# The attention phase of a decoder layer: its ring of PSUM uses on seven banks instead of eight

## The chip, the cores and the metric

One Trainium2 chip, one of its cores. The time is the device time of one execution in microseconds (us), the median of several. Engines are called by the names of the profile: PE (TensorE matmuls), PEld (its weight loads), DVE (VectorE), ACT (ScalarE), POOL (GpSimd), SP (SyncE). PSUM, which PE writes and DVE and ACT read, has eight banks of 128 x 512 fp32 each in this kernel's tensor `ps`.

## The reference, cut to what matters

32 sequences of 128 tokens with 128 features, all fp32:

```
x = layernorm(x + attention(x))              # 16 heads of 64, causal, RoPE on half of each head
x = layernorm(x + cross_attention(x, ctx))   # 16 query heads of 8, 4 key/value heads, masks, RoPE
x = layernorm(x + moe_ffn(x))                # inner x added again; 8 experts, 256 wide, top 2
# attention:  softmax(mask(Q K^T) / 8) V, then W_o
# moe router: softmax-like gates by 3 Sinkhorn rounds over experts and tokens
# expert e:   (relu(x wg[e]) * (x wp[e])) wo[e]
```

## The kernel before, in words

There are two phases. The first does both attentions for all 32 sequences, the second (`ffn_phase`) the experts, in 8 groups of 4 sequences. The change touches the first alone; the second has rings of its own over the same PSUM tensor.

The attention phase is a software pipeline over sequences. `STAGE` gives four stages: f (transpose x, project to Q, K and V, RoPE, transpose heads), k (self-attention scores, softmax, times V, output projection), a (layernorm, cross-attention projections and scores) and c (cross-attention softmax times V, projection, layernorm, router logits). In slot s the sequence s is in stage f, s-1 in k, s-2 in a and s-3 in c. So slots run from 0 to 34: f is on in slots 0 to 31, k in 1 to 32, a in 2 to 33, c in 3 to 34. Slots 0 to 3 and 32 to 34 are written out, slots 4 to 31 are a hardware loop with two slots a turn.

Each engine has its work of a slot as a list in a fixed order (the functions `slot` in the blocks of sync, gpsimd, scalar, vector and tensor), and works it off in order. PE fills a bank, then ACT or DVE empties it. There are 40 such uses of a bank in a slot, listed in PE's order in the argument of `SlotRing`: `c.PT0`, `f.XT`, `c.PT1`, `c.PT2`, `k.S0`, `k.S1`, `f.Q0`, `a.T` and so on. The letter ahead of the point is the stage. Those that matter here:

- `f.XT` is the transpose of x by `x_transpose`, the second thing PE does in a slot. `f.Q0` to `f.Q5` are the projections (`qkv`, three matmuls each at L717 to L719).
- `k.S0` to `k.S3` are the self-attention scores. `scores(u)` fills two of them together and asks for both banks before it issues the first matmul (L738 and then L743). ACT's `exp_fill` empties them, with four exponentials and four reads of the accumulator each (L410), after DVE's `scores_max` (L516).
- `k.PT0` to `k.PT3` are the transposed probabilities (`prob_transpose`, L689), after POOL's `norm_fill` (L336). `k.OT0` and `k.OT1` are the products with V (`pv`, L763), `k.Y` the output projection (`out_proj`, 16 matmuls at L773), which DVE's `residual` (L531) reads.
- `a.QKV` is the cross-attention projection (`xqkv`, L786 and L787). `a.S0` to `a.S3` are the cross-attention scores (`xscores`, L802), emptied by ACT's `xexp_fill`, four exponentials each (L418); the fourth is ACT's last work of a slot.
- `c.PT0` to `c.PT3` are the transposed probabilities of cross-attention (`xprob_transpose`, L689), `c.R` the router logits (`router`, L843).

`SlotRing.bank` puts the use at place i of the list in bank i mod 8. The place is counted anew in every slot, and the list has 40 places. Before PE fills a use it calls `free(name)`, which waits until the bank's previous use has been emptied: the one eight places before, with the last eight of one slot ahead of the first eight of the next. `SlotRing.count` works out the value of the semaphore to wait for, from how often the bank is used in each slot whose stages are on.

Of the kernel before, what the change touches and what calls it, by code (L numbers as in the profile page):

```python
# [30 lines left out]
class Ring:  # L31
# [3 lines left out]
    def __init__(self, sem, name, banks, fills):  # L35
        self.banks = banks
        self.n = len(banks)
        self.per = [len(range(k, fills, self.n)) for k in range(self.n)]
        self.filled = [sem(f"{name}_filled{k}") for k in range(self.n)]
        self.drained = [sem(f"{name}_drained{k}") for k in range(self.n)]  # L40

    def bank(self, fill):
        return self.banks[fill % self.n]

    def count(self, b, fill):
        return b * self.per[fill % self.n] + fill // self.n + 1


class SlotRing:
# [1 line left out]

    def __init__(self, sem, order):
        self.order = order
        self.at = {name: i for i, name in enumerate(order)}
        self.filled = [sem(f"bank_filled{k}") for k in range(8)]
        self.drained = [sem(f"bank_drained{k}") for k in range(8)]
        self.first_full = 3

    def bank(self, name):
        return self.at[name] % 8

    def count(self, s, name):

        i = self.at[name]
        if not isinstance(s, int):
            per = len(range(i % 8, len(self.order), 8))
            return s * per + (self.count(self.first_full, name) - per * self.first_full)
        total = 0  # L70
        for slot in range(s + 1):
            for j in range(i % 8, len(self.order) if slot < s else i + 1, 8):
                if 0 <= slot - STAGE[self.order[j][0]] < B:
                    total += 1
        return total
# [13 lines left out]
def decoder_layer(nc, x, ctx, qmask, kpad, cosq, sinq, xcos, xsin, ident_d, causal_d, gsel_d, wqkv, wo, xwq, xwkv, xwo,  # L89
                  rw, rb, temp, eidx, fwg, fwp, fwo, out):  # L90
    with ExitStack() as whole:
        def sem(name):
            return whole.enter_context(nc.semaphore(name))

        def keep(name, shape, dt=F32):
            return whole.enter_context(nc.sbuf_tensor(name, shape, dt))

        ps = whole.enter_context(nc.psum_tensor("ps", [128, 8, COLS], F32))

        x2_all = keep("x2_all", [128, B, D])  # L100
        x2T_hi = keep("x2T_hi", [128, B * S], F32R)
        x2T_lo = keep("x2T_lo", [128, B * S], F32R)
        logits = keep("logits", [128, B, E])
        ident = keep("ident", [128, 128])
        mhalf = keep("mhalf", [128, FB])
        scratch = keep("scratch", [128, 1])
        eps = keep("eps", [128, FB])
        temp_sb = keep("temp_sb", [128, 1])
        eidx_sb = keep("eidx_sb", [128, E])

        attention_phase(nc, sem, ps, x2_all, x2T_hi, x2T_lo, logits, ident, mhalf, eps, scratch, x, ctx, qmask, kpad, cosq, sinq,
                        xcos, xsin, ident_d, causal_d, gsel_d, wqkv, wo, xwq, xwkv, xwo, rw, rb,
                        [(temp_sb[:], temp), (eidx_sb[:], eidx)])
        ffn_phase(nc, sem, ps, x2_all, x2T_hi, x2T_lo, logits, ident, mhalf, eps, scratch, temp_sb, eidx_sb, fwg, fwp, fwo, out)


def attention_phase(nc, sem, ps, x2_all, x2T_hi, x2T_lo, logits, ident, mhalf, eps, scratch, x, ctx, qmask, kpad, cosq, sinq,
# [4 lines left out]
    with ExitStack() as phase:  # L122
        def sb(name, shape, dt=F32):
# [90 lines left out]

        w_loaded = sem("w_loaded")
        ident_loaded = sem("ident_loaded")
# [177 lines left out]
        def _(act):  # L394
            def copy(s, name, dst, scale=1.0, n=COLS):
                filled(act, s, name)
                nc.scalar.activation(dst, bank(name, n), ACT.Copy, scale=scale).then_inc(ring.drained[ring.bank(name)], 1)  # L397
# [7 lines left out]
            def exp_fill(s, b, n):  # L405

                name = f"k.S{n}"
                act.wait_ge(maxed, 4 * b + n + 1)
                for j in range(4):
                    last = nc.scalar.activation(prob[:, n, j, :], bank(name)[:, j * S:(j + 1) * S], ACT.Exp,  # L410
                                                bias=negmax[:, n, j:j + 1], accum_out=sums[:, n, j:j + 1])
                last.then_inc(ring.drained[ring.bank(name)], 1)

            def xexp_fill(s, b, n):
                name = f"a.S{n}"
                act.wait_ge(xmaxed, 4 * b + n + 1)
                for g in range(XG):
                    last = nc.scalar.activation(xprob[:, n, g, :], bank(name)[:, g * S:(g + 1) * S], ACT.Exp,  # L418
                                                bias=xmax[:, n, g:g + 1])
                last.then_inc(ring.drained[ring.bank(name)], 1)  # L420
# [932 lines left out]
```

## Time and profile before

| what | value |
|---|---|
| median of 3 runs | 1084.07 us (1082.1 to 1084.37) |
| profiled execution, its own time | 1085.77 us |
| span of the profiled execution | 1083.6 us |
| PE busy | 1014.2 us, 94% of the span |
| DVE, ACT, POOL busy | 72%, 63%, 47% |
| mean granted clock of PE | 0.978 |
| attention phase | from the start to about 755 us |

In the rows below the time of a row's start is counted from the start of the span. A row of the timeline may merge several instructions of one kind (`x4`); its second number is then the time from the first's start to the last's end. Matmuls overlap in the pipeline, so a row's end can lie behind the start of the next. What stands in square brackets is how long the engine had been idle and what ended that. The place of a line in kernel.py is written as L689.

### The profile page before, as it was taken

What the parts mean: (1) busy time and instruction counts of PE and PEld (TensorE: products, weight loads), DVE (VectorE), ACT (ScalarE), POOL (GpSimd) and SP (SyncE); (2) the same over time, 40 slices, a digit from 0 to 9 for tenths busy, and PEclk for the clock granted to TensorE, in tenths of its full rate; (3) what the DMA queues carried; (4) which work ended last, traced back from release to release, by engine and by line L of the source; (5) the groups of instructions that cost most, each with busy time, mean ns of one, the idle gap of its engine ahead of it and who ended that gap; (6) DMA issues with size and microseconds to landing.
All of it is one profiled execution on the core that took longest, in us unless ns stands there. A gap on an engine that the chain in (4) does not pass through costs nothing. (4 is left out here: it accounts for less than half of the span.)

```text
span 1083.6 us, 24909 instructions
## 1 busy us (share of the span) xinstructions
PE 1014.2 (94%) x7660; PEld 822.3 (76%) x7692; DVE 776.4 (72%) x2061; ACT 684.8 (63%) x2301; POOL 514.4 (47%) x777
## 2 busy tenths in 40 slices
PE   5999999999999999999999999996499999999996
PEld 3678777777777777777777777774288888888886
DVE  3678888888888888888888888885586445544554
ACT  3788788888888888888888888874322222222221
POOL 4754556545665456654566545640423233323333
PEclk8999999999999999999999999997599999999999
DMA  3000000000000000000000000000300000000000
GB/s 116 9 8 9 11 10 10 7 7 10 12 7 7 7 10 12 7 7 9 8 12 7 7 10 7 7 1 1 117 1 10 1 10 10 10 0 10 10 10 10
DMA packets 22520, 14.46 MB, mean 13 GB/s; under 512 B 3296, under 2 KB 21472, under 8 KB 22240
## 3 DMA queue, kind: packets, MB, share of 16 engines
q1 hardware_dynamic: 22496, 14.15, 4.3%
q8 instruction: 13, 0.21, 0.1%
q14 instruction: 11, 0.09, 0.0%
HBM read 12.05 MB, written 2.10 MB: 13 GB/s over the span
## 5 line engine op out<-in xcount | busy, mean ns | idle before, releaser
L1064 ACT ACTIVATE gs<-ps 128x512 f32<-128x512 f32 x128 | 76.6, 599 | 211.7 <-PE ps L1260 211.7
L410 ACT ACTIVATE prob<-ps,negmax 128x128 f32<-128x128 f32 x512 | 181.4, 416 | 1.2 <-DVE negmax L516 1.2
L418 ACT ACTIVATE xprob<-ps,xmax 128x128 f32<-128x128 f32 x512 | 145.1, 425 | 18.5 <-DVE xmax L516 18.5
L336 POOL TENSOR_TENSOR prob<-prob,recip 128x512 f32<-128x512 f32 x128 | 137.1, 1080 | 35.7 <-DVE recip L521 35.7
L1030 POOL TENSOR_TENSOR acc<-acc,part 128x512 f32<-128x512 f32 x64 | 82.6, 1290 | 142.4 <-DVE part L1193 140.6
L345 POOL TENSOR_TENSOR qk_sin<-qk,sin_sb 128x128 f32<-128x128 f32 x256 | 114.2, 466 | 73.3 <-ACT qk L397 73.0
L410 ACT ACTIVATION_READ_ACCUMULATOR prob<-ps,negmax 128x1 f32 x512 | 131.7, 257 | 0.0
L1268 PEld LDWEIGHTS ps<-fwo_sb,h 128*128 128x128 f32 x1024 | 124.0, 192 | 5.6
L1147 DVE TENSOR_TENSOR h<-ps,gs 128x512 f32<-128x512 f32 x128 | 87.7, 689 | 56.4 <-PE ps L1260 55.3
L1268 PE MATMUL ps<-fwo_sb,h 128*128 128x128 f32 x1024 | 124.4, 275 | 0.0
L360 POOL TENSOR_TENSOR ve<-mv,eps 128x1 f32<-128x1 f32 x64 | 12.1, 189 | 208.4 <-DVE mv L539 208.4
L516 DVE TENSOR_REDUCE xmax<-ps 128x4 f32<-128x512 f32 x128 | 87.2, 688 | 32.0 <-PE ps L802 32.0
L1258 PE MATMUL ps<-x2T_hi,fw_lo 128*128 (+1 forms) x256 | 107.1, 418 | 0.6 <-DVE h L1147 0.6
L351 POOL TENSOR_TENSOR qk<-qk_cos,qk_sin 128x256 f32<-128x256 f32 x128 | 94.5, 739 | 21.2 <-DVE qk_cos L525 21.2
L1260 PE MATMUL ps<-x2T_hi,fw_hi 128*128 (+1 forms) x256 | 102.7, 401 | 0.0
L1259 PE MATMUL ps<-x2T_lo,fw_hi 128*128 (+1 forms) x256 | 101.8, 398 | 0.0
L397 ACT ACTIVATE qk<-ps 128x512 f32<-128x512 f32 x128 | 74.0, 604 | 44.0 <-PE ps L719 43.9
L1193 DVE TENSOR_TENSOR part<-ps,wts 128x512 f32<-128x512 f32 x64 | 44.1, 691 | 74.1 <-PE ps L1268 74.0
L516 DVE TENSOR_REDUCE negmax<-ps 128x4 f32<-128x512 f32 x128 | 85.0, 685 | 14.2 <-PE ps L743 14.1
L717 PE MATMUL ps<-w_lo,xT_hi 128*128 128x512 f32 x192 | 91.1, 475 | 1.2 <-DVE xT_lo L550 1.2
L689 PE MATMUL ps<-ident,prob 128*128 128x128 f32 x512 | 78.5, 276 | 11.6 <-POOL prob L336 9.1
L743 PEld LDWEIGHTS ps<-kT,qT 64*128 64x128 f32 x1024 | 62.9, 189 | 27.5 <-issue 27.5
(158 smaller groups left out, 2377.5 us busy)
## 6 DMA issues: line engine op xcount, KB each, us to landing
xf<-in_x SPq DMA_DIRECT2D x32, 64.0 KB, 1.8
xres<-in_x SPq DMA_DIRECT2D x32, 64.0 KB, 1.8
cx<-in_ctx SPq DMA_DIRECT2D x32, 64.0 KB, 1.8
out_y<-yo SPq DMA_DIRECT2D x8, 256.0 KB, 2.3
fstage<-in_fwg SPq DMA_DIRECT2D x1, 1024.0 KB, 5.4
fstage<-in_fwp SPq DMA_DIRECT2D x1, 1024.0 KB, 7.6
qk<-in_wqkv SPq DMA_DIRECT2D x1, 768.0 KB, 4.7
prob<-in_wqkv SPq DMA_DIRECT2D x1, 768.0 KB, 6.7
```

What stands on the lines that cost most here:

```text
L336: nc.gpsimd.tensor_tensor(prob[:, n], prob[:, n], recip[:, n, :, None].broadcast_to([128, 4, S]), ALU.mult).then_inc(normed, 1)
L345: last = nc.gpsimd.tensor_tensor(sines[:, :, side, :], part[:, :, 1 - side, :], table, ALU.mult)
L351: nc.gpsimd.tensor_tensor(qk[:, 8 * n:8 * n + 8, 0:ROPE], qk_cos[:, 8 * n:8 * n + 8, :], qk_sin[:, 8 * n:8 * n + 8, :], ALU.add).then_inc( ...
L410: last = nc.scalar.activation(prob[:, n, j, :], bank(name)[:, j * S:(j + 1) * S], ACT.Exp, bias=negmax[:, n, j:j + 1], accum_out=sums[:, n ...
L418: last = nc.scalar.activation(xprob[:, n, g, :], bank(name)[:, g * S:(g + 1) * S], ACT.Exp, bias=xmax[:, n, g:g + 1])
L516: nc.vector.tensor_reduce(dst, bank(name).rearrange("p (j s) -> p j s", j=4), AX_X, ALU.max, negate=True).then_inc(done, 1)
L717: nc.tensor.matmul(dst, xT_hi[:], w_lo[:, cols], start=True, stop=False)
L1147: nc.vector.tensor_tensor(h[n % 4][:], ps[:, up.bank(2 * n + 1), :], gs[n % 2][:], ALU.mult)\
L1258: nc.tensor.matmul(dst, w_lo[i][:, cols], hi, start=True, stop=False)
L1259: nc.tensor.matmul(dst, w_hi[i][:, cols], lo, start=False, stop=False)
L1260: nc.tensor.matmul(dst, w_hi[i][:, cols], hi, start=False, stop=True).then_inc(up.filled[fill % 4], 1)
L1268: last = nc.tensor.matmul(ps[:, down.bank(e), b * D:(b + 1) * D], h[n % 4][:, b * S:(b + 1) * S], wo_sb[:, n, :], start=(n % 2 == 0), stop ...
```

## The change

The ring gets the number of its banks as an argument, and the attention phase passes 7. The use at place i of the list is then in bank i mod 7; bank 7 is in no use of this phase. The waits follow by the same rule. As 40 is no multiple of 7 (it is 5 x 7 + 5), the distance is seven places within a slot but not over the border of two slots. There the first seven uses follow, in their banks, on `a.S2`, `a.S3`, `c.XT`, `k.Y`, `c.R`, `f.T2` and `f.T3` of the slot before. On eight banks the first eight follow on `k.OT1`, `f.T2`, `f.T3`, `a.S2`, `a.S3`, `c.XT`, `k.Y` and `c.R`. No instruction that computes or moves data is added or removed, and the order on each engine stays.

```diff
-    def __init__(self, sem, order):
+    def __init__(self, sem, order, banks):
         self.order = order
+        self.n = banks
         self.at = {name: i for i, name in enumerate(order)}
-        self.filled = [sem(f"bank_filled{k}") for k in range(8)]
-        self.drained = [sem(f"bank_drained{k}") for k in range(8)]
+        self.filled = [sem(f"bank_filled{k}") for k in range(banks)]
+        self.drained = [sem(f"bank_drained{k}") for k in range(banks)]
...
     def bank(self, name):
-        return self.at[name] % 8
+        return self.at[name] % self.n
...
         if not isinstance(s, int):
-            per = len(range(i % 8, len(self.order), 8))
+            per = len(range(i % self.n, len(self.order), self.n))
             return s * per + (self.count(self.first_full, name) - per * self.first_full)
         total = 0
         for slot in range(s + 1):
-            for j in range(i % 8, len(self.order) if slot < s else i + 1, 8):
+            for j in range(i % self.n, len(self.order) if slot < s else i + 1, self.n):
...
-            "k.OT1", "f.T2", "f.T3", "a.S2", "a.S3", "c.XT", "k.Y", "c.R"])
+            "k.OT1", "f.T2", "f.T3", "a.S2", "a.S3", "c.XT", "k.Y", "c.R"], 7)
```

## Rows read from the trace of the kernel before

**Rows 1.** The page's busy times: engine, us, share of the span, instructions.

```profile
PE 1014.2 (94%) x7660; PEld 822.3 (76%) x7692; DVE 776.4 (72%) x2061; ACT 684.8 (63%) x2301; POOL 514.4 (47%) x777
```

**Rows 2.** Busy us by stretch: length, PE, PEld, DVE, ACT, POOL, granted clock, DMA.

```profile
160.00:360.00 200.00, 194.99 (x1626) 154.41 (x1636) 166.32 (x474) 164.64 (x592) 110.71 (x188) 1.00 0.03 9
...
741.00:748.00 7.00, 4.46 (x21) 3.13 (x20) 5.51 (x17) 4.62 (x18) 0.74 (x2) 0.77 0.00 0
748.00:755.00 7.00, 5.21 (x24) 3.08 (x22) 2.08 (x3) 1.46 (x4) 0.00 (x0) 0.50 0.00 0
```

**Rows 3.** Waits from 50 to 720 us: total us, times, longest us.

```profile
PE ps L689 <- POOL prob L336: 9.1, 29, 0.3
PE ps L689 <- DVE xq_pad L608: 7.5, 30, 0.9
```

**Rows 4.** Timeline of PE, end of slot 14 and start of slot 15.

```profile
309.60 0.63 PE L689 MATMUL ps<-ident,xprob 128*128 128x128 f32 x4
...
326.49 0.50 PE L802 MATMUL ps<-xkT,xqT 128*128 128x512 f32 x1
...
330.12 1.95 PE L773 MATMUL ps<-wo_sb,oT 128*128 128x128 f32 x16
...
332.04 0.64 PE L689 MATMUL ps<-ident,xprob 128*128 128x128 f32 x4
332.51 0.27 PE L689 MATMUL ps<-ident,xf 128*128 128x128 f32 x1
332.62 1.04 PE L689 MATMUL ps<-ident,xprob 128*128 128x128 f32 x8
```

**Rows 5.** Timeline of ACT, end of slot 14.

```profile
327.75 1.14 ACT L418 ACTIVATE xprob<-ps,xmax 128x128 f32<-128x128 f32 x4 [0.55 <-DVE xmax L516]
...
329.24 1.17 ACT L418 ACTIVATE xprob<-ps,xmax 128x128 f32<-128x128 f32 x4
...
330.71 2.24 ACT L418 ACTIVATE xprob<-ps,xmax 128x128 f32<-128x128 f32 x8
```

**Rows 6.** Timeline of PE, early in slot 14.

```profile
314.83 0.60 PE L738 MATMUL ps<-causal,identb 128*128 128x512 bf16 x2
...
316.46 0.49 PE L786 MATMUL ps<-xwq_sb,xcT 128*128 128x128 f32 x2
...
317.43 0.66 PE L689 MATMUL ps<-ident,prob 128*128 128x128 f32 x4 [0.32 <-POOL prob L336]
```

**Rows 7.** Timeline of ACT, early in slot 14.

```profile
313.67 0.60 ACT L397 ACTIVATE qk<-ps 128x512 f32<-128x512 f32 x1 [1.16 <-PE ps L719]
...
315.44 0.22 ACT L410 ACTIVATION_READ_ACCUMULATOR prob<-ps,negmax 128x1 f32 x1
...
316.81 0.25 ACT L410 ACTIVATION_READ_ACCUMULATOR prob<-ps,negmax 128x1 f32 x1
```

**Rows 8.** Timeline of POOL, slot 14.

```profile
316.26 1.04 POOL L336 TENSOR_TENSOR prob<-prob,recip 128x512 f32<-128x512 f32 x1 [1.04 <-DVE recip L521]
```

**Rows 9.** Timeline of slot 1: a wait of PE for an emptied bank.

```profile
22.54 0.60 ACT L397 ACTIVATE kT<-ps 128x512 f32<-128x512 f32 x1 [4.40 <-PE ps L689]
...
23.39 1.01 PE L738 MATMUL ps<-causal,identb 128*128 128x512 bf16 x2 [0.67 <-ACT kT L397]
```

**Rows 10.** Timeline of DVE, slots 14 and 15.

```profile
310.64 0.29 DVE L531 TENSOR_TENSOR y<-ps,xres 128x128 f32<-128x128 f32 x1 [0.40 <-issue]
...
321.42 0.69 DVE L495 COPY v<-ps 128x512 f32<-128x512 f32 x1 [0.19 <-PE ps L719]
...
332.66 0.29 DVE L531 TENSOR_TENSOR y<-ps,xres 128x128 f32<-128x128 f32 x1
```

**Rows 11.** Timeline of ACT and PE, slot 14, around `k.OT0`.

```profile
324.65 0.59 ACT L397 ACTIVATE probT<-ps 128x512 f32<-128x512 f32 x1
...
325.47 1.09 PE L763 MATMUL ps<-probT,v 128*64 128x128 f32 x16
```

**Rows 12.** Timeline of slot 32, PE and ACT.

```profile
718.36 0.59 PE L738 MATMUL ps<-causal,identb 128*128 128x512 bf16 x2
...
719.63 0.21 ACT L410 ACTIVATION_READ_ACCUMULATOR prob<-ps,negmax 128x1 f32 x1
...
721.39 0.63 PE L689 MATMUL ps<-ident,prob 128*128 128x128 f32 x4 [0.76 <-ACT prob L410]
```

## The prediction

> **What bounds the kernel now.** I read the page's busy times first: PE is busy 94% of the span, no other engine over 72% [rows 1]. Then the table by stretch: from 160 to 360 us PE works 194.99 of 200 us at granted clock 1.00, DVE 166, ACT 165 [rows 2]. So in the steady slots PE sets the pace, and what makes PE wait is paid in full unless PE waits later in the same slot for something that has not moved. Then the list of waits, to see how much there is to absorb: PE has two waits a slot, 9.1 us / 29 = 0.31 us for POOL's normalised probabilities and 7.5 / 30 = 0.25 us for DVE's padded queries [rows 3]. Last the timelines of slot 14, which stands for the others: its first row is at 309.60 and the next slot's at 332.04, 22.44 us apart [rows 4].
>
> **The change, part by part.** It adds and removes no work; it moves the target of PE's waits from eight uses back to seven. For each of the 40 uses I set PE's first matmul of it beside the end of the emptying instruction it will wait for. Most keep room: `f.Q0` after `f.T3` or `f.Q3` after `f.Q1` have microseconds. Six do not have it clearly.
>
> What does it take from an end to PE's next matmul? Two rows bound it. POOL's multiplication ends at 316.26 + 1.04 = 317.30 and PE, waiting for it, starts at 317.43: 0.13 us [rows 6, 8]. In slot 1 PE waits for a bank in the very `scores` call that matters here: ACT ends at 22.54 + 0.60 = 23.14, PE starts at 23.39: 0.25 us [rows 9]. I take 0.13 for a transpose and 0.25 for `scores`, and keep both as ends.
>
> *Wait A, the turn of the slot.* `f.XT` is at place 1 and will follow `a.S3`, ACT's last work of the slot before. PE starts it at 332.51 [rows 4]. ACT finishes `a.S3` at 330.71 + 2.24 = 332.95 [rows 5]. The new start is 332.95 + 0.13 = 333.08, or 0.57 us late (0.69 with 0.25). ACT can't be earlier: its chain there begins with PE's `a.S0` at 326.49 and an idle stretch of 0.55 that ends with DVE's maximum, and runs nearly without a gap to the end [rows 4, 5]. It moves with PE, so the loss returns every slot. Behind `f.XT` are `c.PT1`, `c.PT2`, the scores and the projections; ACT, which now idles 1.16 us for `f.Q0` [rows 7], gets all of it later by the same amount. That is why nothing is won back.
>
> Part of A comes earlier. `k.Y` will follow `a.S1`, which ends at 329.24 + 1.17 = 330.41 [rows 5], while PE starts `k.Y` at 330.12 [rows 4]: 0.42 us late. This puts `f.XT` at 332.93, and the rest of A is 0.15. The two overlap; together they are 0.57, not 0.99.
>
> *Wait B, the second pair of scores.* `k.S3`, place 11, will follow `k.S0`, place 4; on eight banks it follows `c.PT2`, long since empty by then. `scores(1)` asks for both its banks before its first matmul, at 314.83 [rows 6]. ACT finishes with `k.S0` at 315.44 + 0.22 = 315.66 [rows 7]. The new start is 315.66 + 0.25 = 315.91: 1.08 us late (0.96 with 0.13). Behind it on PE is `a.QKV`, which will follow `k.S1`: free at 316.81 + 0.25 = 317.06 [rows 7], while PE reaches it at 316.46 + 1.08 = 317.54. That wait is hidden by B; without B it would be 0.73. Next is `k.PT0`, for which PE idles 0.32 today. POOL's work ends at 317.30 in both kernels, since it hangs on `k.S0` alone [rows 6, 8]. So 0.32 is absorbed and B costs 1.08 - 0.32 = 0.76 (0.64 with 0.13).
>
> Does B's delay grow or shrink afterwards? ACT and DVE get `k.S2` and `k.S3` about 1 us later, but DVE waits for PE again at `f.Q4` (0.19 idle at 321.42) [rows 10], ahead of the padded queries, so that wait of 0.25 moves along and absorbs nothing.
>
> *Near misses.* `c.PT2` will follow `k.Y`, emptied by DVE at 332.66 + 0.29 = 332.95, and in even slots, where DVE turns its loop, at 310.64 + 0.29 = 310.93 [rows 10]. PE reaches it with the fifth of the eight transposes that start at 332.62, 0.11 apart: 333.06, which is 1.02 after the slot's first row, so 310.62 in the even slot [rows 4]. With A it is 0.57 later, 311.19: 0.26 after DVE's end, less 0.13. `k.OT0` will follow `k.PT2`: ACT ends at 324.65 + 0.59 = 325.24, PE starts at 325.47 [rows 11]: 0.23, less 0.13. Both at nothing; if the cover goes, each costs 0.1 to 0.3 us a slot.
>
> *How often.* A needs stage f in the slot and stage a in the one before: slots 3 to 31, 29 times. B needs stage k: those 29, and slots 1, 2 and 32. In slot 32 ACT frees `k.S0` at 719.63 + 0.21 = 719.84, PE wants it at 718.36, and 0.76 is absorbed [rows 12]: 719.84 + 0.25 - 718.36 - 0.76 = 0.97. I count 2.5 us for the three. After slot 32, and in the expert phase of some 324 us, nothing changes.
>
> *The sum.* 29 x (0.57 + 0.76) = 38.6, and 2.5: 41 us. On the profiled execution's 1085.77 us (span 1083.6 and 2.2 around it) that is 1126.9. The median shown lies 1.7 us lower, so the forecast is 1125 us. With 0.13 for both it is 29 x 1.21 + 2 = 37 us, 1121; with 0.25 for both 29 x 1.45 + 2.5 = 44.5 us, 1129.
>
> *The clock.* Between 160 and 360 us, with two waits a slot, the granted clock is 1.00, its level of 2.4 GHz. Late in the drain of the pipeline, after a stretch with PE busy 4.46 of 7 us, it is 0.50, the level of 1.2 GHz [rows 2]. With A and B PE would still work some 21.9 us (194.99 / 200 of 22.44) of 23.8. The Trainium skill, in "TensorE: Matmul & The Clock Gate", section "A second HAM failure mode: psum-queue depth-cycling", says that a kernel which cycles through its PSUM banks can idle in small pieces often enough that the clock falls and rises again and again. The rows of before speak against it; it is a rival below.
>
> **The rivals.**
> - *More near misses bite.* `c.PT2` and `k.OT0` come into play, or the first matmuls after a stall are slower because no weights are loaded ahead. 0.2 to 0.4 us a slot over 29 slots is 6 to 12 us more: 1131 to 1137. For it: margins of 0.10 and 0.13 that are left. Against it: the rows of slot 14 leave both just free.
> - *Only one of A and B costs.* If PE's recorded start at `scores(1)` hides slack, only A is paid: 29 x 0.57 = 16.5, 1101. If ACT comes to the end of the slot earlier than its rows say, because PE's pauses leave it alone, only B is paid: 29 x 0.76 + 2.5 = 24.5, 1109.
> - *The clock falls.* This is a mechanism of the kernel: a stall of 0.4 us or more at two places a slot, beside the two that stand. A slot has 21.9 us of PE work at full clock; 7 us of a slot at half clock do the work of 3.5. Once a slot, 29 times, that is about 100 us: 1225.
> - *Not slower.* The present two waits, 0.56 us a slot, would have to swallow all. This needs ACT to be done with `k.S0` by 314.83 + 0.31, half a microsecond earlier, and with `a.S3` by 332.38. ACT's exponentials would have to run about a quarter faster. Then the time stays at 1084, and if the new order also spares PE a part of those waits, up to 29 x 0.3 = 9 us less. The decision lies at 315.1 for the end of `k.S0`. Against it: nothing of ACT's chain to it changes, and ACT starts it only after `f.Q0`, which PE brings.
> - *The change does nothing,* since PE waits only where data are late. Against it: in each of the two places the end of the emptying lies behind PE's start, by 0.44 and 0.83 us, before any delay is added.
>
> **How the numbers follow.** Forecast 0.63 (1117 to 1130); more near misses 0.18; only one of the two 0.12; the clock 0.03; not slower, or nothing, 0.04. The range takes the forecast, most of the near misses and the upper of the single waits: 1109 to 1139. A measurement of this kernel tells 0.2%, some 2 us, from no change. All cases but the last are slower by far more: slower 0.96, same 0.03, faster 0.01.
>
> **What the profile of the changed kernel would show.** A slot of about 23.8 us from the first `xprob` transpose to the next. PE idle ahead of the transpose of `xf` (about 0.15) and of `out_proj` (about 0.4), ended by ACT's `xprob`. PE idle of about 1 us ahead of L738, ended by ACT's `prob`. No more wait of 0.32 for POOL at `k.PT0`. Granted clock still 1.00 up to slot 32. The expert phase as long as before. I am wrong if the idle time ahead of L738 is well off 1 us, if the wait at `k.PT0` is still there, if new waits stand at `c.PT2` or `k.OT0`, or if the clock shows half level inside the loop.

## The result, and the profile after

| | before | changed |
|---|---|---|
| median | 1083.09 us (1081.42 to 1084.37, 4 runs) | 1113.28 us (1112.66 to 1115.32, 4 runs) |
| profiled execution, its span | 1085.77, 1083.6 us | 1115.32, 1113.1 us |
| mean granted clock | 0.978 | 0.978 |

The ratio is 1.0283, with a 95% interval of 1.0261 to 1.0304: 30.2 us slower, where 41 were forecast (1125, range 1109 to 1139). The direction and the two waits were right, the size of one of them was not. The time is inside the stated range, but below the 1117 to 1130 that the prediction gave to its forecast proper.

The page's busy times, and the same stretch of the table by stretch as in [rows 2]:

```profile
PE 1025.4 (92%) x7660; PEld 818.8 (74%) x7692; DVE 777.9 (70%) x2061; ACT 686.6 (62%) x2301; POOL 516.4 (46%) x777
...
160.00:360.00 200.00, 190.71 (x1563) 146.79 (x1568) 161.22 (x455) 159.32 (x580) 109.75 (x183) 1.00 0.03 9
```

The counts over the whole span are those of [rows 1]: the work is the same. In 200 us PE does less of it, 190.71 against 194.99 us busy, and the clock is still 1.00. PE's waits from 50 to 750 us (total us, times, longest us) answer to [rows 3]:

```profile
PE ps L739 <- ACT prob L411: 22.9, 30, 1.6
PE ps L774 <- ACT xprob L419: 8.3, 30, 0.4
PE ps L690 <- DVE xq_pad L609: 0.6, 1, 0.6
PE ps L690 <- ACT prob L411: 0.5, 1, 0.5
```

Two new waits stand there 30 times each: 0.76 us ahead of the second pair of scores (B), 0.28 us ahead of the output projection (A, at `k.Y`). Both old ones, for POOL and for DVE's padded queries, are gone or nearly gone. So PE's idle time does not simply grow by B and A. Next PE's timeline, slot 15 from its first row to that of slot 16, the slot that answers to [rows 4, 6]:

```profile
344.19 0.63 PE L690 MATMUL ps<-ident,xprob 128*128 128x128 f32 x4
344.66 0.32 PE L690 MATMUL ps<-ident,xf 128*128 128x128 f32 x1
344.82 1.04 PE L690 MATMUL ps<-ident,xprob 128*128 128x128 f32 x8
...
350.36 0.61 PE L739 MATMUL ps<-causal,identb 128*128 128x512 bf16 x2 [0.73 <-ACT prob L411]
...
352.31 0.33 PE L788 MATMUL ps<-xwkv_sb,xcT 128*128 128x64 f32 x2
352.48 0.61 PE L690 MATMUL ps<-ident,prob 128*128 128x128 f32 x4
...
358.40 0.66 PE L690 MATMUL ps<-ident,xq_pad 128*128 128x128 f32 x4
...
365.40 2.02 PE L774 MATMUL ps<-wo_sb,oT 128*128 128x128 f32 x16 [0.27 <-ACT xprob L419]
...
367.40 0.63 PE L690 MATMUL ps<-ident,xprob 128*128 128x128 f32 x4
```

The same slot of the kernel before starts at 332.04 and ends, with the first row of slot 16, at 354.56:

```profile
337.28 0.60 PE L738 MATMUL ps<-causal,identb 128*128 128x512 bf16 x2
...
339.23 0.33 PE L787 MATMUL ps<-xwkv_sb,xcT 128*128 128x64 f32 x2
339.88 0.65 PE L689 MATMUL ps<-ident,prob 128*128 128x128 f32 x4 [0.32 <-POOL prob L336]
...
346.06 0.65 PE L689 MATMUL ps<-ident,xq_pad 128*128 128x128 f32 x4 [0.24 <-DVE xq_pad L608]
...
352.63 1.95 PE L773 MATMUL ps<-wo_sb,oT 128*128 128x128 f32 x16
...
354.56 0.63 PE L689 MATMUL ps<-ident,xprob 128*128 128x128 f32 x4
```

Each row's start, counted from its slot's first row, gives how late PE is at each place:

| place | before | changed | late by |
|---|---|---|---|
| `scores(1)` | 5.24 | 6.17 | 0.93 |
| `k.PT0` | 7.84 | 8.29 | 0.45 |
| `a.QT`, the padded queries | 14.02 | 14.21 | 0.19 |
| `k.Y` | 20.59 | 21.21 | 0.62 |
| next slot | 22.52 | 23.21 | 0.69 |

B makes PE 0.88 us late (0.05 come from the transpose of `xf`), and by the padded queries all but 0.14 of that is back. A then adds 0.50: 0.43 ahead of `k.Y`, and 0.07 because the output projection itself runs longer (2.02 against 1.95). In slot 14, an even one, there is a third piece. Its first row is at 320.73, and `scores(0)` starts 1.97 us later, where it is 1.67 in slots 14 and 15 of before: 0.05 from `xf`, and 0.25 because the fifth of the eight transposes, `c.PT2`, waits for DVE to empty `k.Y`, at 321.64 + 0.29 = 321.93. The slot lasts 23.46 us against 22.44.

```profile
321.37 1.27 PE L690 MATMUL ps<-ident,xprob 128*128 128x128 f32 x8
...
321.64 0.29 DVE L532 TENSOR_TENSOR y<-ps,xres 128x128 f32<-128x128 f32 x1 [0.47 <-issue]
```

### The profile page after: what moved, and what is told of

Its sections match the earlier page's. It is cut to its first block and busy times, and to the rows that moved or that the text cites. A ratio compares the mean times of both kernels' runs of the same rounds, so it can differ in the third digit from the quotient of the medians.

```text
span 1113.1 us, 24939 instructions
## 1 busy us (share of the span) xinstructions
PE 1025.4 (92%) x7660; PEld 818.8 (74%) x7692; DVE 777.9 (70%) x2061; ACT 686.6 (62%) x2301; POOL 516.4 (46%) x777
## 5 line engine op out<-in xcount | busy, mean ns | idle before, releaser
L337 POOL TENSOR_TENSOR prob<-prob,recip 128x512 f32<-128x512 f32 x128 | 133.0, 1040 | 42.7 <-DVE recip L522 38.5
L411 ACT ACTIVATION_READ_ACCUMULATOR prob<-ps,negmax 128x1 f32 x512 | 113.4, 221 | 0.0
```

Source lines behind the costliest of these rows:

```text
L337: nc.gpsimd.tensor_tensor(prob[:, n], prob[:, n], recip[:, n, :, None].broadcast_to([128, 4, S]), ALU.mult).then_inc(normed, 1)
```

## The experiments

The bank of each use can be set by name in all of them. This is the common edit; what follows shows only the names that were given another bank.

```diff
-    def __init__(self, sem, order, banks):
+    def __init__(self, sem, order, banks, moved):
...
+        self.of = [moved.get(name, i % banks) for i, name in enumerate(order)]
...
-        return self.at[name] % self.n
+        return self.of[self.at[name]]
...
-            per = len(range(i % self.n, len(self.order), self.n))
+            per = self.of.count(self.of[i])
...
-            for j in range(i % self.n, len(self.order) if slot < s else i + 1, self.n):
-                if 0 <= slot - STAGE[self.order[j][0]] < B:
+            for j in range(len(self.order) if slot < s else i + 1):
+                if self.of[j] == self.of[i] and 0 <= slot - STAGE[self.order[j][0]] < B:
```

**B alone, on eight banks.**

```diff
+ 8, {"k.S3": 4, "a.QKV": 3}
```

> The kernel before, on eight banks, with wait B alone: k.S3 goes to bank 4, where it follows k.S0, and a.QKV to bank 3, where it follows c.PT2. All other uses keep their previous use or one that is emptied earlier still. Theory 1 (B is largely swallowed: in the changed kernel's slot 15 scores(1) starts 0.9 us late, k.PT0 0.4, the padded queries 0.2): 29 x 0.2 and about 3 for slots 1, 2 and 32, so some 9 us, 1092 (1089 to 1095). Theory 2 (the prediction's step: B costs 0.76 a slot): 29 x 0.76 + 2.5 = 24.5, 1107. Theory 3 (what costs is the number of banks, not which use follows which): no change, 1083.

1092.37 us against 1084.31, ratio 1.0079 (1.0062 to 1.0096): 8.1 us. Theory 1 holds; the prediction's price of 24.5 does not. The slots last 22.70 us where those of before last 22.50, and PE waits for little else:

```profile
PE ps L741 <- ACT prob L413: 22.7, 30, 1.5
PE ps L692 <- DVE xq_pad L611: 1.8, 2, 1.1
```

So 22.7 us of idle time ahead of one line cost 8 us, since the two waits of [rows 3] are gone in exchange.

**A alone, on eight banks.** `f.XT` behind `a.S3`.

```diff
+ 8, {"f.XT": 4, "f.Q1": 4, "f.Q4": 4, "f.T0": 4, "k.S0": 1, "a.QKV": 1, "f.Q5": 1, "k.OT0": 1}
```

> The kernel before, on eight banks, with wait A alone: f.XT follows a.S3, since the uses at places 1, 9, 17 and 25 go to bank 4 and those at 4, 12, 20 and 28 to bank 1; k.Y stays behind f.T1. Theory 1 (A costs what the rows give, and nothing swallows it): a.S3 is empty 0.44 after f.XT's old start, and with 0.05 to 0.13 behind it 29 x 0.49 to 0.57 = 14 to 16.5 us, 1097 to 1100. Rival (A is swallowed like B by PE's later waits for POOL and DVE): 0 to 5 us, 1083 to 1088. Theory 3 (the number of banks costs): no change, 1083.

1096.02 us against 1084.31, ratio 1.0124 (1.0098 to 1.0149): 11.7 us. Not swallowed, as theory 1 says, though 1 us under its range. The steady slots are 0.5 us longer (23.0), which is 15 us for 29. What is missing goes with the clock outside the steady slots. From 22 to 26 us, in slot 1, the granted clock of the kernel before is 0.50, the level of 1.2 GHz; with A alone it is 1.00. In the 4 us from 16 to 20 PE had been busy 1.98 and 1.95 us, much the same. First before, then A alone:

```profile
22.00:26.00 4.00, 3.33 (x22) 2.10 (x20) 0.40 (x2) 0.77 (x2) 0.00 (x0) 0.50 0.06 16
22.00:26.00 4.00, 3.85 (x29) 2.52 (x32) 2.00 (x4) 1.30 (x7) 0.62 (x1) 1.00 0.06 16
```

Three of the four executions of A alone have a mean granted clock of 0.986 (1095.2 to 1096.2 us). The fourth has 0.980 and took 1099.97 us, 14.5 to 16.5 more than the eight executions of the kernel before at 0.978 and 0.979. The one of before at 0.987 took 1079.02, 16 to 17 less than the three. So at like clocks A costs some 15 to 17 us. Here the waits for POOL stay, since nothing comes between the scores and `k.PT0`:

```profile
PE ps L692 <- ACT xprob L421: 10.3, 29, 0.7
PE ps L692 <- POOL prob L339: 9.1, 29, 0.3
PE ps L692 <- DVE xq_pad L611: 3.9, 15, 0.9
```

**The changed kernel without B.**

```diff
+ 7, {"k.S3": 6, "a.QKV": 4, "k.PT0": 5}
```

> The changed kernel, on seven banks, without wait B: k.S3 goes to bank 6 behind f.Q0, a.QKV to bank 4 behind k.S0, k.PT0 to bank 5 behind k.S1. A and the near miss at c.PT2 stay. Theory 1 (B is worth some 9 us): 1113 - 9 = 1104 (1101 to 1107), with the wait of about 0.3 us for POOL at k.PT0 back in its place. Theory 2 (B is worth 24.5): 1089. Theory 3: 1113.

1106.58 us (1105.51 to 1107.89), 6.7 less than the changed kernel: again B's price is about a third of the forecast. Theory 1's range is met. The wait for POOL is back with the same sum as before the change (`PE ps L692 <- POOL prob L339: 9.1, 29, 0.3`).

**Seven banks, other pairs.** Here is what the forecast's method gives when it is turned round: each use gets the bank in which the use before it is long empty.

```diff
+ 7, {"c.PT0": 5, "f.XT": 1, "c.PT1": 2, "c.PT2": 3, "k.S0": 6, "k.S1": 0, "f.Q0": 4, "a.T": 3, "c.PT3": 5,
+     "f.Q1": 2, "k.S2": 3, "k.S3": 1, "a.QKV": 4, "k.PT0": 5, "f.Q2": 0, "c.OT": 6, "f.Q3": 4, "f.Q4": 3,
+     "k.PT1": 1, "c.O": 2, "f.Q5": 6, "k.PT2": 5, "a.QT": 0, "a.KT": 4, "c.T": 3, "f.T0": 6, "k.PT3": 2,
+     "c.Y": 1, "k.OT0": 3, "a.S0": 0, "f.T1": 4, "a.S1": 5, "k.OT1": 1, "f.T2": 2, "f.T3": 6, "a.S2": 3,
+     "a.S3": 0, "c.XT": 1, "k.Y": 4, "c.R": 6}
```

> Seven banks, with a bank for each of the 40 uses chosen from the times in the trace of before, so that the previous use of its bank is emptied at least 0.4 us before PE's first matmul in both kinds of slots. Bank 7 is free as in the changed kernel. Theory 1 and 2 (only the pairs of uses cost, not the number of banks): as before, 1083 (1081 to 1085). Theory 3 (seven banks are too few for the amount of work in flight): 1105 or more, near the changed kernel's 1113.

1084.19 us against 1084.31, ratio 1.0002 (0.9993 to 1.0012). All 30 us are gone, and bank 7 is still free. From 160 to 360 us PE is as busy as in [rows 2]:

```profile
160.00:360.00 200.00, 195.63 (x1636) 154.66 (x1639) 166.22 (x468) 165.54 (x591) 109.63 (x186) 1.00 0.03 9
```

So seven banks are not too few; counting modulo 7 pairs the wrong uses.

**The near miss at `c.PT2` alone.**

```diff
+ 7, {"c.R": 3, "k.OT1": 3, "k.Y": 4, "a.S1": 4}
```

> The changed kernel with c.PT2 behind c.R instead of k.Y, and k.S0 behind k.Y; to get there k.OT1 and c.R go to bank 3, a.S1 and k.Y to bank 4. A and B stay as they are. Theory 1 (the near miss at c.PT2 costs 0.25 us in each even slot, where DVE turns its loop before it empties k.Y): 14 x 0.25 = 3.5 less, 1109.5 (1108 to 1112), and even slots as long as odd ones. Rival (the even slots are longer for PE's own turn of the loop): 1113.

1111.45 us (1109.95 to 1112.45) against 1083.62 of before in the same runs: about 2 us less than the changed kernel, in the range of theory 1 but too little to be told from noise by itself. The trace is clearer: even slots last 23.25 us and no longer 23.46, odd ones 23.19.

**The two parts of A.**

```diff
+ 7, {"k.Y": 4, "c.R": 3}
```

> The changed kernel with k.Y and c.R in each other's banks: k.Y (bank 4) follows k.OT1 and no longer a.S1, c.R (bank 3) follows a.S1, and c.PT2 now follows c.R. f.XT still follows a.S3. Theory 1 (k.Y's wait and f.XT's are one wait, since ACT's last exponential sets both): the wait moves from k.Y to f.XT, 0.5 us a slot as before, and what is won is only the 3.5 us of c.PT2: 1109 to 1111. Rival (the two add up, and k.Y's share of 0.5 is saved): 29 x 0.5 less as well, about 1095.

1107.89 us (1107.51 to 1109.57), 5.4 less than the changed kernel, not 18. That is 1 us under the range of theory 1, and far from the rival's 1095. `k.Y` starts on time, and `f.XT` starts 0.49 us later instead and takes 0.05 longer: one wait in two places, as the prediction had it. All slots last 23.1 to 23.2 us.

**More work for PE ahead of `k.PT0`, on both kernels.**

```diff
-                if on(k):
-                    prob_transpose(0)
                 if on(f):
                     qkv(2)
+                if on(k):
+                    prob_transpose(0)
```

> The kernel before on eight banks, with PE's order changed at one place: the projection f.Q2 (0.8 us of PE) is issued before k.PT0 and not after it; the banks of both stay what they were. Theory 1 (the start of k.PT0 lies 0.47 us later than PE could have it, which is what swallowed half of B): PE has work for that time, and up to 29 x 0.47 = 14 us are won, less if the padded queries, which PE reaches sooner, wait longer: 1069 to 1079. Rival (PE's idle time there was only the 0.32 us of the row, or the later waits give it all back): 1079 to 1084.

> The changed kernel with the same reordering, f.Q2 before k.PT0, the banks of both unchanged. Theory 1 (B's delay already fills the wait at k.PT0): nothing left to win there, 1113 (1110 to 1114), against a gain in the same step of the kernel before. Rival (the wait at k.PT0 is independent of B): the same gain as on eight banks, 1100 to 1105.

On eight banks 1082.79 us against 1083.62, ratio 0.9985 (0.9971 to 1.0000); on seven 1113.35, the changed kernel's time. The second is as expected, the first is not: theory 1 wanted 5 to 14 us and got less than 1, so the rival's second half holds, that the later waits give it all back. `k.PT0` and all up to `k.PT2` did move, the latter by 0.47 us, and at the padded queries it was given back. There the PE wait from 50 to 740 us is now 20.7 us in total, where the kernel before has 8.3:

```profile
PE ps L692 <- DVE xq_pad L611: 20.7, 31, 0.9
```

It shows where B's second part went. DVE's work on the padded queries (four instructions, L603 to L608 in the kernel before) does not end earlier when PE is early. Groups by line from 110 to 690 us (count | busy us, mean ns), first of the kernel before, then of this one, then of the changed one:

```profile
L603 DVE SCALAR_TENSOR_TENSOR xq_pad<-xr,qm,xq_pad 128x128 fp32r<-128x128 f32 x26 | 16.1, 619 | 0.0
L605 DVE TENSOR_TENSOR xk_pad<-xr,xk_pad 128x32 fp32r<-128x32 f32 x26 | 11.7, 449 | 0.0
L607 DVE CAST xk_pad<-kb_all 128x4 fp32r x26 | 11.0, 423 | 0.0
L608 DVE CAST xq_pad<-qm 128x16 fp32r<-128x16 f32 x26 | 5.5, 210 | 0.0
```

```profile
L606 DVE SCALAR_TENSOR_TENSOR xq_pad<-xr,qm,xq_pad 128x128 fp32r<-128x128 f32 x26 | 28.6, 1101 | 0.0
L608 DVE TENSOR_TENSOR xk_pad<-xr,xk_pad 128x32 fp32r<-128x32 f32 x26 | 11.4, 438 | 0.0
L611 DVE CAST xq_pad<-qm 128x16 fp32r<-128x16 f32 x26 | 11.3, 434 | 0.0
L610 DVE CAST xk_pad<-kb_all 128x4 fp32r x26 | 4.1, 158 | 0.0
```

```profile
L604 DVE SCALAR_TENSOR_TENSOR xq_pad<-xr,qm,xq_pad 128x128 fp32r<-128x128 f32 x25 | 11.8, 472 | 0.0
L608 DVE CAST xk_pad<-kb_all 128x4 fp32r x25 | 11.8, 472 | 0.0
L606 DVE TENSOR_TENSOR xk_pad<-xr,xk_pad 128x32 fp32r<-128x32 f32 x25 | 11.2, 447 | 0.0
L609 DVE CAST xq_pad<-qm 128x16 fp32r<-128x16 f32 x25 | 4.2, 169 | 0.0
```

The sums of the four means are 1.70, 2.13 and 1.56 us: with PE 0.47 early DVE takes 0.43 longer, with PE late it takes 0.14 less. What holds DVE is seen beside POOL, in slot 14 of the kernel with `f.Q2` ahead:

```profile
319.39 2.04 POOL L339 TENSOR_TENSOR prob<-prob,recip 128x512 f32<-128x512 f32 x2
...
320.48 1.10 DVE L606 SCALAR_TENSOR_TENSOR xq_pad<-xr,qm,xq_pad 128x128 fp32r<-128x128 f32 x1
```

POOL ends at 321.43, DVE at 321.58, 0.15 behind. In the kernel before it is the same 0.15, 322.64 behind 322.49:

```profile
320.46 2.03 POOL L336 TENSOR_TENSOR prob<-prob,recip 128x512 f32<-128x512 f32 x2
...
322.03 0.61 DVE L603 SCALAR_TENSOR_TENSOR xq_pad<-xr,qm,xq_pad 128x128 fp32r<-128x128 f32 x1
```

Both ends are as far from the start of their slot in the two kernels (POOL's 12.89 and 12.90 us), though DVE began 0.48 earlier in the second. With B alone and in the changed kernel DVE's first instruction also ends 0.15 behind POOL's.

**Less work for POOL.** To see whether POOL's run sets that wait, a part of it was left out, in the kernel before and in the one with B alone. Both then leave three of four heads of the last multiplication unscaled, and their results are not those of the reference.

```diff
-                nc.gpsimd.tensor_tensor(prob[:, n], prob[:, n], recip[:, n, :, None].broadcast_to([128, 4, S]),
+                h = 1 if n == 3 else 4
+                nc.gpsimd.tensor_tensor(prob[:, n, 0:h], prob[:, n, 0:h], recip[:, n, 0:h, None].broadcast_to([128, h, S]),
```

> The kernel before on eight banks, in which POOL's last multiplication of a slot by the reciprocals (norm_fill of k.S3) works on one head in place of four, so some 0.8 us of POOL's run from k.S0 to the padded queries is left out (part of the probabilities stays unscaled). Theory 1 (PE's wait at the padded queries is set by POOL's unbroken run, behind which DVE's work on them ends; it swallowed 0.2 of B): PE reaches a.QT 0.4 us sooner in each slot, 29 x 0.42 = 12 us less, 1072 (1069 to 1076). Rival (DVE or ACT sets that wait): 1081 to 1084.

> The same shortened multiplication, with wait B alone on eight banks (k.S3 behind k.S0, a.QKV behind c.PT2). Theory 1: only k.PT0 still swallows a part of B, so B costs 0.89 - 0.47 = 0.42 a slot, 29 x 0.42 and 3: 15 us over the kernel with the shortened multiplication alone, 1087 (1084 to 1090), where B cost 8 on the kernel before. Rival (what swallows B does not hang on POOL): again 8 over it.

Without B 1083.82 us against 1083.77, ratio 1.0001 (0.9991 to 1.0011): nothing won, a miss for theory 1. With B 1098.29, 14.5 us over it: the difference that theory 1 wanted, and the rival's 8 is out (theory 1's 1087 itself missed with the gain it was counted from). The traces tell why both came true. The first of the four instructions, L607 here, fell to 383 ns, but the third now meets POOL's next one and is held in its place. First without B, then with it:

```profile
321.06 0.72 POOL L355 TENSOR_TENSOR qk<-qk_cos,qk_sin 128x256 f32<-128x256 f32 x1
...
321.07 0.74 DVE L611 CAST xk_pad<-kb_all 128x4 fp32r x1
...
329.05 0.74 POOL L355 TENSOR_TENSOR qk<-qk_cos,qk_sin 128x256 f32<-128x256 f32 x1
...
329.07 0.74 DVE L611 CAST xk_pad<-kb_all 128x4 fp32r x1
```

The end of DVE's work is bound to the end of some POOL instruction, not to the one that I shortened. How much of B is swallowed there depends on how far that POOL instruction moves with PE. `f.XT` starts at 308.44 in this slot without B and at 316.06 with it. So POOL's row comes 12.62 and 12.99 us after it, 0.37 later with B, as much as the slot is longer (22.90 against 22.53): nothing is swallowed. In the kernels with the full multiplication POOL's run ends 12.42 us after `f.XT` without B and 12.64 with B alone, 0.22 later, and the slot is 0.20 longer. That POOL takes part is shown; that the shortened multiplication alone sets the wait is refuted.

**Both gaps filled, on eight banks.** First `f.T0` alone ahead of the padded queries, then with `f.Q2` and `k.PT3` as well. The second's list of PE's work, where it differs (banks unchanged):

```diff
-            "c.PT3", "f.Q1", "k.S2", "k.S3", "a.QKV", "k.PT0", "f.Q2", "c.OT",
+            "c.PT3", "f.Q1", "k.S2", "k.S3", "a.QKV", "f.Q2", "k.PT0", "c.OT",
-            "f.Q3", "f.Q4", "k.PT1", "c.O", "f.Q5", "k.PT2", "a.QT", "a.KT",
-            "c.T", "f.T0", "k.PT3", "c.Y", "k.OT0", "a.S0", "f.T1", "a.S1",
+            "f.Q3", "f.Q4", "k.PT1", "c.O", "f.Q5", "k.PT2", "f.T0", "k.PT3",
+            "a.QT", "a.KT", "c.T", "k.OT0", "c.Y", "a.S0", "f.T1", "a.S1",
```

> The kernel before on eight banks, with f.T0 (0.44 us of PE, ready long before) issued ahead of a.QT, a.KT and c.T and not behind them; banks unchanged. Theory 1 (PE stands for 0.39 to 0.46 us at the padded queries): the gap is filled, up to 29 x 0.42 = 12 us less, 1072 (1071 to 1077), unless ACT or DVE becomes the bound at the end of the slot. Rival (the gain is given back at a later wait, as that of f.Q2 was): 1081 to 1084.

> Eight banks, with both gaps of PE filled: f.Q2 ahead of k.PT0, and f.T0 and k.PT3 ahead of a.QT; so that c.Y has something ahead of it, it follows k.OT0. Theory 1 (each slot has 0.47 and 0.42 us in which PE could work): up to 29 x 0.89 = 26 us less, 1058, and more likely 1058 to 1070, since with a period under 22 us DVE and ACT (18.6 us of work a slot) have less room at the turn of the slot. Rival (another wait takes their place at once): 1075 to 1084.

1076.88 us for the first, ratio 0.9937 (0.9912 to 0.9962), and 1064.1 us for the second, 0.9802 (0.9768 to 0.9836), against 1083.77. The first won 7 of the 12 us that were expected: slots of 22.26 us, so 0.24 and not 0.42 a slot (`c.Y`, with less work ahead of it, is complete 0.42 us after `k.PT3` where it was 0.22). The second won 20: slots of 21.80 us, and PE's records leave no gap at all:

```profile
160.00:360.00 200.00, 200.00 (x1690) 159.87 (x1689) 174.62 (x485) 168.76 (x610) 116.07 (x196) 1.00 0.03 9
```

This version beats both kernels. `f.Q2` ahead of `k.PT0` is worth under 1 us by itself, and `f.T0` alone 7; how the 20 divide among `f.Q2`, `f.T0`, `k.PT3` and `c.Y`, which all moved in the second, is not shown.

## Why the prediction was right, and where its size was off

- **PE sets the pace.** Right: with PE's gaps filled a slot is 0.70 us shorter, 20.3 for 29, and the kernel is 19.7 us faster.
- **Wait A, 0.57 us a slot, in two overlapping parts.** Right: 0.43 ahead of `k.Y` (0.42 forecast), 0.07 in its longer run and 0.05 at `f.XT`. Alone it lengthens slots by 0.5 us, and with `k.Y` freed it moves to `f.XT` instead of shrinking. For 29 slots, 16 us of the forecast's 16.5.
- **Wait B, 1.08 - 0.32 = 0.76 a slot.** This is the term that was mis-sized. It cost 0.14 in slot 15 and 0.19 in slot 14, some 5 us where 22 stood in the sum. Three parts of its working failed:
  - *The step from ACT's end to PE's start.* I took 0.25 us from slot 1. ACT ends with `k.S0` at 350.08 + 0.23 = 350.31 and PE starts at 350.36: 0.05, and 0.05 or 0.06 in every slot from 4 to 31. That is 0.2 a slot.
  - *What the wait at `k.PT0` absorbs.* I took the idle time of the row, 0.32. It absorbed 0.48. From start to start, L787 to `k.PT0`, it was 0.65 (339.23 to 339.88) and became 0.17: matmuls overlap, and idle time is counted from the modelled end of the one before. That is 0.16 a slot.
  - *"That wait of 0.25 moves along and absorbs nothing."* DVE waits for PE ahead of the padded queries, as I wrote, but the instructions behind that wait end with POOL's. Going from 0.45 to 0.19 late, PE got 0.26 us back by there, and in slot 14 0.22.
  - Together 1.08 - 0.20 - 0.48 - 0.26 = 0.14, the measured value of slot 15.
- **`a.QKV` behind `k.S1` is hidden by B.** PE reaches it at 351.99, and ACT's `k.S1` ends before (four readings 0.34 apart after 350.31, so 351.7). Right.
- **Near misses at nothing.** Half wrong: `k.OT0` stayed free, but `c.PT2` costs 0.25 us in even slots, 14 x 0.25 = 3.5 us. I set PE's delay against DVE's old end and forgot that A makes `k.Y`, and so DVE, late too. A new wait at `c.PT2` was one of the signs of being wrong that the prediction named.
- **Slots 1, 2 and 32, 2.5 us.** Too small: slot 32 alone lasts 2.45 us longer (19.16 to 21.61), since PE waits again behind `scores(1)`, 1.78 us at `k.PT1` and 1.00 at `k.Y`. `k.PT1` follows `k.S3` on seven banks, a pair that has room in the steady slots and that the prediction did not look at here. Slots 1 and 2 last 2.9 us longer, but they also differ between kernels that should not differ there, so of the three I give no more than about 5 us.
- **The sum.** For slots 3 to 31 the parts give 29 x 0.55 + 29 x 0.17 + 3.5 = 24.4 us, and the traces 24.3. The other 5 us of the difference of 29.5 in span are read off, not worked out: 5.4 in slots 1, 2 and 32, 1.1 less before slot 1, and 0.9 behind slot 32 that I can't place.
- **The rivals.** Of "more near misses" `c.PT2` came true, and yet the time was below the forecast. Its other half is true in small: `k.Y` and `f.XT` take 0.07 and 0.05 us longer behind their stall. "Only one of A and B costs" has two halves. B costs little, as its first half says, but not for slack at `scores(1)`, and its 1101 is 12 us too low. Its second half, B alone at 1109, was nearest in time and is wrong.
- **What was luck.** The forecast proper had 1117 to 1130, and 1113 is outside. The stated range holds the result only because its lower end was taken from the rival with B alone, which did not happen.
- **The clock.** In the changed kernel it stayed at 1.00, 2.4 GHz, from 28 us to behind slot 32, through all stalls of the steady slots. From 22 to 26 us it was 0.50 in both kernels, after PE had been busy 1.98 (before) and 1.12 (changed) of the 4 us from 16 to 20. The mean over the whole execution is 0.978 in both, so the clock does not explain the difference. By the Trainium skill's "A second HAM failure mode: psum-queue depth-cycling" in "TensorE: Matmul & The Clock Gate" it could have gone up and down, and the trace disagrees for stalls of this size, 0.8 and 0.3 us in every slot.

## What to carry to other kernels

In a ring of buffers it is the pairs that cost: for each use, set the start of its fill beside the end of the emptying that it will wait for, and choose the buffer by that; a plain modulo changes all pairs when the count changes. Measure what a later wait can absorb from start to start on the waiting engine, compare it with the same work where nothing waits, and follow it to the end of the slot: a delay is a cost only if it is still there at the last place where the engine waits. The same waits are an offer to the tuner: work that is ready, put into every one of them at once, won 20 us where the first alone won less than one.

## What the runs showed of the hardware

- A DVE instruction that runs beside POOL's can end with it. Small ones on the padded queries, 128 x 128 and less, take 383 to 1101 ns in mean for the same shape, and end 0.15 us (the first of them, in four kernels) or 0.03 us (the cast, 321.81 after 321.78) behind the end of a POOL instruction. The Trainium skill, "SBUF — State Buffer", section "Who interferes with whom", says that a DVE instruction with two inputs in SBUF contends with a POOL instruction that reads SBUF, and that the ports they share are an exclusive lock. The trace agrees for L603, 0.15 us behind in both kernels. Why the cast, with one input, is held too is not shown.
- From the end of ACT's last read of a bank to PE's first matmul into it there were 0.05 us in the steady slots and 0.15 in slots 2, 3 and 32 of the changed kernel, which are written out, not the 0.25 of slot 1. ACT's row in slot 15 of the changed kernel ends at 350.31, and PE's, shown above, starts at 350.36:

```profile
350.08 0.23 ACT L411 ACTIVATION_READ_ACCUMULATOR prob<-ps,negmax 128x1 f32 x1
```
